# A group's residual moved into the next group's first step, and its token statistics spread over that group's later steps

## The chip, the core and the metric

The kernel runs on one core of a Trainium2 chip. Its time is the device time of one execution, in microseconds (us). Five engines work side by side and meet at semaphores: PE (TensorE, matmuls; its weight loads are listed as PEld), DVE (VectorE), ACT (ScalarE), POOL (GpSimd) and SP (SyncE, which here issues the DMAs).

## The reference

The model has two layers, each a gated cross attention and a gated feed-forward part, over x of 128 batches x 64 tokens x 128 features. The change lies in the feed-forward part of layer 0, a mixture of 16 experts in which each expert chooses 32 tokens of every batch:

```python
gates, idx = jax.lax.top_k(affinity, CAP)                 # CAP = 32 tokens per expert and batch
expert_in = jnp.take_along_axis(x[:, None, :, :], idx[..., None], axis=2)
h = jax.nn.gelu(jnp.einsum('becd,edf->becf', expert_in, w1) + b1[None, :, None, :])
expert_out = jnp.einsum('becf,efd->becd', h, w2) + b2[None, :, None, :]
out = out.at[jnp.arange(b)[:, None, None], idx].add(gates[..., None] * expert_out)
```

Around it stands `x = x + tanh(g_ffn[0]) * ffn(layernorm(x))`, and the attention of layer 1 begins with a layernorm of the new x.

## The kernel before

x stays on the chip as 64 tiles of 128 tokens. The expert stage, `run_experts`, cuts the 128 batches into 8 groups of 16 (8 tiles, 512 chosen rows for each expert). A group goes through the 16 experts one after another, so the stage is a pipeline of 128 steps. `body(a)` issues, on every engine, what belongs to one step `j`; `a.e` is the step's number in its group, from 1 to 16.

On PE a step has four parts, in this order: two `take` matmuls that gather rows of the next group (L1428, into `psR` and `psH`); 12 matmuls of the first layer of expert j+1 (L231, `psH`), called H here; 48 matmuls of the second layer of expert j (L231, `psE`), called E; and 16 that add the result of expert j-1 back to the tokens (L1503, `psA`), called A. In a group's first step eight matmuls seed `psA` with the bias (L1496). `psE` and `psA` have one buffer each.

On DVE a step is, in this order: a copy of gathered rows (L1582, `xg`); the gating of E's result, `psE` times the gate into `eo32` (L1615, semaphore `gated`); four `put` matrices (L1622); the low half of h (L1604); the low half of `eo` (L1630); and the other low half of h (L1604). Every second step also normalises a tile: L1563, L1577 and at its end L1568. ACT does the other copy of gathered rows, two pairs of Gelus (L1544) each followed by the high half of h (L1549), and the high half of `eo` (L1539).

Each engine takes its instructions in the order in which they are written, so three waits matter here. E of step j waits for `gated` of step j-1, because `psE` must be read before it is written again. A waits for `put` and `eo_lo`. The bias matmuls wait for `xadd`, which says that the group before has been read out of `psA`.

`residual(G)` runs on DVE alone, between step 16 of group G and step 1 of the next one. It waits for the group's last A, adds `psA` times the gate to the group's 8 tiles of x in two instructions (L1642), and then computes `bn_stats` for each of the 8 tiles (L176), which the layernorm of layer 1 will read after the stage.

`all_steps` writes steps -1 and 0 out, then loops over groups 0 to 5 (a `Fori` over G) with an inner loop of four steps a turn for steps 3 to 14, and writes groups 6 and 7 out (their inner loops stay). The last two groups gather little or nothing for a next one.

Of the kernel before, what the change touches and what calls it, by code (L numbers as in the profile page):

```python
# [24 lines left out]
NE, CAP, DFF = 16, 32, 512  # L25
# [78 lines left out]
def _build(nc, whole, I, out):  # L104
# [36 lines left out]
    x = sb(whole, "x", [P, NT, D], F32)  # L141
# [32 lines left out]
    def queue_stats(e, t):  # L174

        return e.bn_stats(tile_of(t, stats), tile_of(t, x))  # L176
# [1107 lines left out]
    def run_experts(tag, gate, ew, idx16, gate_slot, tok_slot):  # L1284
# [11 lines left out]
        GT = GB * N // P  # L1296
# [3 lines left out]
        with ExitStack() as c:  # L1300
# [71 lines left out]
                parity = (at.G + 1 + (at.k // GT if at.i is None else 0)) & 1  # L1372
                return [gathered(parity, at.bp, (k % GT if at.i is None else k) * 2 + side) for side in range(2)]

            def all_steps(eng, body, after_group):

                def group(G):
                    for k in (1, 2):
                        body(At(G, k))

                    fours = (NE - 4) // 4 - (isinstance(G, int) and G == NG - 2)
                    with eng.Fori(0, fours) as i:
                        for u in range(4):
                            body(At(G, 3 + u, i))
                    for k in range(3 + 4 * fours, NE + 1):
                        body(At(G, k))
                    after_group(G)
                for k in (-1, 0):
                    body(At(0, k))
                with eng.Fori(0, NG - 2) as G:  # L1390
                    group(G)
                for G in (NG - 2, NG - 1):
                    group(G)

            with nc.Block() as block:
# [23 lines left out]
                def _(e):  # L1419
# [25 lines left out]
                    def body(a):  # L1445
# [41 lines left out]
                        if a.has(-1):  # L1487
# [16 lines left out]
                                                        start=False,  # L1504
                                                        stop=a.e == NE and hl == 1, skip_group_check=True)
                            last.then_inc(s["A"], 1)
                    all_steps(e, body, lambda G: None)

                @block.scalar
                def _(e):  # L1510
                    for k in range(GT + 1):
                        t = Step(None, 0, k)
                        wait(e, s["ln"], t)
                        wait(e, s["g"], t - 2, 2)
                        e.activation(xn[:, k % 2, 0], xnf[:, k % 2], ACT.Copy).then_inc(s["x_hi"], 1)
                        if k < GT:
                            for hl in range(2):
                                wait(e, s["g"], t, 2, hl - 1)
                                e.activation(gathered(0, hl, 2 * k + 1),
                                             psH[:, 2 * hl + 1, :].rearrange("p (e c) -> p e c", c=CAP), ACT.Copy)\  # L1520
                                 .then_inc(s["g_1"], 1)

                    def body(a):
                        j, par = a.j, a.par

                        if a.has_tile(0):
                            wait(e, s["g"], a.t, 2, a.bp - 1)
                            e.activation(rows_of(a)[1], psH[:, 3, :].rearrange("p (e c) -> p e c", c=CAP), ACT.Copy)\
                             .then_inc(s["g_1"], 1)
                        for ft in range(FT):  # L1530
                            if ft == 2 and a.bp == 1 and a.has_tile(1):
                                tpar = (a.k + 1) % 2
                                wait(e, s["ln"], a.t + 1)
                                wait(e, s["g"], a.t - 1, 2)
                                e.activation(xn[:, tpar, 0], xnf[:, tpar], ACT.Copy).then_inc(s["x_hi"], 1)
                            if ft == 2 and a.has(-1):
                                wait(e, s["gated"], j - 1)
                                wait(e, seeded["A"], j - 2)
                                e.activation(eo[:, 0], eo32[:], ACT.Copy).then_inc(s["eo_hi"], 1)  # L1539
                            if a.has(1):  # L1540
                                wait(e, s["H"], j + 1, FT, ft + 1 - FT)
                                if ft % 2 == 0:
                                    wait(e, s["h_lo"], j, 2, ft // 2 - 1)
                                e.activation(g32[:, ft, :], psH[:, ft, :], ACT.Gelu_apprx_tanh,  # L1544
                                             bias=b1T[:, bass.ds(a.expert(1) * FT + ft, 1)]).then_inc(s["gelu"], 1)
                                if ft % 2 == 1:
                                    wait(e, s["gelu"], j + 1, FT, ft + 1 - FT)
                                    wait(e, s["E"], j - 1)
                                    e.activation(h[:, 1 - par, 0, ft - 1:ft + 1, :], g32[:, ft - 1:ft + 1, :],  # L1549
                                                 ACT.Copy).then_inc(s["h_hi"], 1)  # L1550
                    all_steps(e, body, lambda G: None)

                @block.vector
                def _(e):
# [6 lines left out]
                    def queue_tile(t, par):  # L1561
                        wait(e, s["x_lo"], t - 2)
                        e.tensor_scalar(xnf[:, par], tile_of(t, x), column_of(t, mean), column_of(t, rstd),  # L1563
                                        ALU.subtract, ALU.mult).then_inc(s["ln"], 1)
# [31 lines left out]
                    def body(a):  # L1596
                        j, par = a.j, a.par
                        next_tile = a.bp == 1 and a.has_tile(1)

                        def h_low(q):  # L1600
                            if a.has(1):
                                wait(e, s["h_hi"], j + 1, 2, q - 1)
                                wait(e, s["E"], j - 1)
                                e.tensor_tensor(h[:, 1 - par, 1, 2 * q:2 * q + 2, :], g32[:, 2 * q:2 * q + 2, :],  # L1604
                                                h[:, 1 - par, 0, 2 * q:2 * q + 2, :], ALU.subtract)\
                                 .then_inc(s["h_lo"], 1)

                        if a.has_tile(0):
                            gathered_rows(a.t, a.bp, rows_of(a)[0], psR[:])
                        if a.has(-1):  # L1610
                            wait(e, s["E"], j - 1)
                            wait(e, s["eo_lo"], j - 2)
                            g4 = gate_slot[:, bass.ds(a.expert(-1), 1), bass.ds(a.group(-1) * RT, RT)]\
                                .rearrange("p o r -> p (o r)")
                            e.tensor_tensor(eo32[:], psE[:], g4.unsqueeze(2).broadcast_to([P, RT, D]),  # L1615
                                            ALU.mult).then_inc(s["gated"], 1)
                        if next_tile:
                            queue_tile(a.t + 1, (a.k + 1) % 2)
                        if a.has(-1):
                            wait(e, seeded["A"], j - 2)  # L1620
                            for r in range(RT):
                                e.tensor_scalar(put[:, r, :], iota[:],  # L1622
                                                tok_slot[:, bass.ds(a.expert(-1), 1),
                                                         bass.ds(a.group(-1) * RT + r, 1)]
                                                .rearrange("p o r -> p (o r)"),
                                                None, ALU.is_equal).then_inc(s["put"], 1)
                        h_low(0)
                        if a.has(-1):
                            wait(e, s["eo_hi"], j - 1)
                            e.tensor_tensor(eo[:, 1], eo32[:], eo[:, 0], ALU.subtract)\  # L1630
                             .then_inc(s["eo_lo"], 1)
                        if next_tile:
                            select(a.t + 1, (a.k + 1) % 2, False)
                        h_low(1)
                        if next_tile:
                            split_tile(a.t + 1, (a.k + 1) % 2)

                    def residual(G):
                        wait(e, seeded["A"], At(G, NE - 1).j)
                        for q in range(2):  # L1640
                            xs = x[:].rearrange("p (t h) d -> p t h d", h=2)[:, bass.ds(G * RT, RT), q, :]
                            last = e.scalar_tensor_tensor(xs, psA[:, q], gate, xs, ALU.mult, ALU.add)  # L1642
                        last.then_inc(s["xadd"], 1)
                        wait(e, seeded["xadd"], flat(G, 1, None, 0, 0))
                        for k in range(GT):
                            queue_stats(e, flat(G, GT, None, 0, k))
                    all_steps(e, body, residual)
        s.close()


# [350 lines left out]
```

## Time and profile before

| | us |
|---|---|
| median of 3 runs | 2259.38 |
| lowest and highest | 2254.52 and 2264.16 |
| the profiled execution | 2259.92 |
| its span | 2258.2 |

The time of the profiled execution is 1.72 us longer than its span. In the page's list of busy time PE is busy for 2070.6 us (92% of the span), DVE for 1746.0 us (77%), ACT for 1598.8 us (71%) and POOL for 653.8 us (29%). The expert stage lies between about 575 and 1466 us. In the rows below an engine's start and duration are in us from the start of the span, and the granted clock of TensorE is a share of full speed, so 1.00 is 2.4 GHz and 0.50 is 1.2 GHz.

### The profile page before, as it was taken

Reading aid. Unit: us, or ns where it says so; the run is one execution under the profiler, and the core shown is the slowest. Engines: PE = TensorE matmul, PEld = TensorE weight load, DVE = VectorE, ACT = ScalarE, POOL = GpSimd, SP = SyncE. Lnnn points to the kernel's source line nnn. Section 1 sums busy time; section 2 is a strip of 40 time slices with the busy share of each in tenths; the row PEclk is TensorE's granted clock in tenths of the full one; section 3 lists DMA queues with packets and bytes.
Section 4 is the critical chain, followed back from the end, with each engine's and each line's share of the span. In section 5 each row is a group of like instructions: output and inputs, shape, how many; then the busy total and the mean of one; then the engine's idle time right before and its main releaser. Section 6 shows DMA issues by size and latency. Waiting matters only on the chain. (4 is left out here: it accounts for less than half of the span.)

```text
span 2258.2 us, 74593 instructions
## 1 busy us (share of the span) xinstructions
PE 2070.6 (92%) x26251; PEld 1394.0 (62%) x26251; DVE 1746.0 (77%) x3815; ACT 1598.8 (71%) x2792; POOL 653.8 (29%) x890
## 2 busy tenths in 40 slices
PE   6999999675799999999999999879999999999798
PEld 4666666433366666666666667656666666667566
DVE  4888887578787878787878787678888888888644
ACT  4777777454687888888878887656666667777533
POOL 3666666401000000000000000035455554444454
PEclk8999999777799999999999999989999999999899
DMA  7011110247000000000000000031111110000133
GB/s 173 27 32 31 32 32 26 53 172 279 12 10 11 9 11 12 10 11 11 9 11 9 12 8 2 0 91 61 58 57 59 60 52 7 4 4 5 41 103 103
DMA packets 105107, 96.64 MB, mean 43 GB/s; under 512 B 35920, under 2 KB 90048, under 8 KB 104640
## 3 DMA queue, kind: packets, MB, share of 16 engines
q1 hardware_dynamic: 104464, 95.51, 13.8%
q8 instruction: 45, 0.74, 0.1%
q14 instruction: 38, 0.31, 0.0%
q10 hardware_dynamic: 560, 0.08, 0.0%
HBM read 56.00 MB, written 31.10 MB: 39 GB/s over the span
## 5 line engine op out<-in xcount | busy, mean ns | idle before, releaser
L1604 DVE TENSOR_TENSOR h<-g,h 128x1024 f16<-128x1024 f32 x256 | 313.7, 1225 | 173.0 <-ACT h L1549 171.5
L231 PE MATMUL psE<-ew,h 128*128 (+1 forms) x6144 | 389.5, 223 | 31.7 <-DVE eo L1615 30.4
L231 PEld LDWEIGHTS psE<-ew,h 128*128 128x128 f16 x6144 | 370.9, 100 | 75.8 <-issue 28.8
L231 PE MATMUL psH<-xg,ew 128*128 (+1 forms) x1536 | 354.8, 381 | 2.4 <-issue 1.8
L1544 ACT ACTIVATE g<-psH,eb1T 128x512 f32<-128x512 f32 x512 | 322.5, 679 | 36.5 <-PE psH L231 27.0
L570 PE MATMUL psV<-Bw,cT 96*64 96x512 f16 x2064 | 288.0, 386 | 3.9 <-DVE vB L749 3.9
L723 POOL TENSOR_TENSOR E<-E,rden 128x512 f32<-128x512 f32 x192 | 200.4, 1044 | 292.6 <-DVE rden L758 292.6
L1549 ACT ACTIVATE h<-g 128x1024 f16<-128x1024 f32 x256 | 270.9, 1058 | 18.0 <-ACT g L1544 1.5
L714 POOL TENSOR_TENSOR Ph<-E,Ph 128x512 f16<-128x512 f32 x192 | 222.4, 1158 | 181.2 <-ACT Ph L674 181.2
L1662 POOL MEMSET rbias<- 64x384 f32 x1 | 0.4, 412 | 910.5 <-POOLq L132 910.5
L655 ACT ACTIVATE vB<-psV 128x512 f16<-128x512 f32 x344 | 202.9, 590 | 78.5 <-PE psV L570 78.5
L231 PEld LDWEIGHTS psH<-xg,ew 128*128 (+1 forms) x1536 | 144.0, 98 | 182.6 <-issue 35.2
L231 PE MATMUL psU<-cT,AT 96*128 96x128 f16 x3648 | 241.6, 222 | 13.3 <-DVE vB L749 11.9
L231 PEld LDWEIGHTS psU<-cT,AT 96*128 96x128 f16 x3648 | 208.9, 99 | 34.4 <-issue 11.2
L749 DVE TENSOR_TENSOR vB<-psV,vB 128x512 f16<-128x512 f32 x344 | 226.9, 659 | 0.4 <-ACT vB L655 0.4
L640 PE MATMUL psS<-u,xTa 128*64 128x256 f32 x1536 | 210.7, 396 | 2.0 <-ACT u L692 1.6
L692 ACT ACTIVATE u<-psU 128x512 f32<-128x512 f32 x304 | 180.8, 595 | 38.0 <-PE psU L231 30.8
L763 DVE COPY PT<-psT 128x1024 f16<-128x1024 f16 x192 | 132.4, 690 | 78.1 <-PE psT L627 77.9
L766 DVE TENSOR_REDUCE top<-psS 128x8 f32<-128x512 f32 x192 | 132.4, 690 | 64.3 <-PE psS L640 64.3
L606 PEld LDWEIGHTS psY<-vB,PT 128*64 128x64 f16 x4608 | 144.8, 110 | 34.3 <-DVE PT L763 11.8
L606 PE MATMUL psY<-vB,PT 128*64 128x128 f16 x4608 | 163.1, 220 | 1.6 <-DVE PT L763 1.6
L686 ACT ACTIVATE E<-E,zero_col 128x512 f32<-128x512 f32 x192 | 138.3, 720 | 25.5 <-DVE E L769 25.5
(253 smaller groups left out, 3121.0 us busy)
## 6 DMA issues: line engine op xcount, KB each, us to landing
keys_ahead<-ust SPq DMA_DIRECT2D x40, 512.0 KB, 4.8
u<-keys_ahead SPq DMA_DIRECT2D x40, 512.0 KB, 3.4
rawe<-in_L_ffn_w_dram SPq DMA_DIRECT2D x32, 256.0 KB, 2.7
wb<-rw SPq DMA_DIRECT2D x64, 128.0 KB, 2.0
rows<-places SPq DMA_DIRECT2D x110, 64.0 KB, 2.6
out_dram<-x SPq DMA_DIRECT2D x7, 512.0 KB, 3.2
context_T<-cT SPq DMA_DIRECT2D x64, 48.0 KB, 1.5
cT<-context_T SPq DMA_DIRECT2D x64, 48.0 KB, 1.7
```

Of the source, the lines that this page charges most:

```text
L231: last = e.matmul(to, a, b, start=start and n == 0, stop=stop and n == 2, **flags)
L570: last = e.matmul(a.values(b)[half(hp)], cT[:, a.ring, cl, half(b)], Bw[:, bl, a.g, hp].rearrange("p k d -> p (k d)"), start=n == 0, stop= ...
L606: last = e.matmul(psY[half(b), 0:D], PT[:, a3.par, pl, pair, half(b)], vB[:, a3.par, vl, b, pair, :], start=a3.g == n == pair == 0, stop=a ...
L640: last = e.matmul(psS[half(b), h:h + 4, :], xT[:, a.tp, half(b)], u[:, a.slot, h:h + 4, half(b)], start=True, stop=True)
L655: e.activation(vB[:, a.par, 0, b].rearrange("p k d -> p (k d)"), a.values(b), ACT.Copy).then_inc(s["vh" + name], 1)
L692: e.activation(u[:, a.slot, 4 * b:4 * b + 4].rearrange("p h l -> p (h l)"), psU[:, b, :], ACT.Copy).then_inc(s[f"uc{b}"], 1)
L714: e.tensor_tensor(Ph[:, a2.par, 1].rearrange("p k t -> p (k t)"), E[:, a2.par].rearrange("p h l -> p (h l)"), Ph[:, a2.par, 0].rearrange(" ...
L723: e.tensor_tensor(E[:, a1.par], E[:, a1.par], rden[:, a1.par, :].unsqueeze(2).broadcast_to([P, 8, N]), ALU.mult)\
L749: e.tensor_tensor(vB[:, a.par, 1, b].rearrange("p k d -> p (k d)"), a.values(b), vB[:, a.par, 0, b].rearrange("p k d -> p (k d)"), ALU.sub ...
L1544: e.activation(g32[:, ft, :], psH[:, ft, :], ACT.Gelu_apprx_tanh, bias=b1T[:, bass.ds(a.expert(1) * FT + ft, 1)]).then_inc(s["gelu"], 1)
L1549: e.activation(h[:, 1 - par, 0, ft - 1:ft + 1, :], g32[:, ft - 1:ft + 1, :], ACT.Copy).then_inc(s["h_hi"], 1)
L1604: e.tensor_tensor(h[:, 1 - par, 1, 2 * q:2 * q + 2, :], g32[:, 2 * q:2 * q + 2, :], h[:, 1 - par, 0, 2 * q:2 * q + 2, :], ALU.subtract)\
```

## The change

`residual` is split in two. The additions to x for group G-1 now stand in step 1 of group G, behind that step's gating (L1615) and ahead of its `put` instructions. The eight statistics of group G-1 stand at the end of later steps of group G: two at the end of step 2, and one each at the end of steps 3, 5, 7, 9, 11 and 13. After the last group both parts run as before. Since group 0 has no group before it, its steps are written out ahead of the loop, which now runs over groups 1 to 5.

```diff
-            def all_steps(eng, body, after_group):
+            def all_steps(eng, body):
...
-                    after_group(G)
                 for k in (-1, 0):
                     body(At(0, k))
-                with eng.Fori(0, NG - 2) as G:
+                group(0)
+                with eng.Fori(1, NG - 2) as G:
                     group(G)
...
                         if next_tile:
                             queue_tile(a.t + 1, (a.k + 1) % 2)
+                        if a.e == 1 and a.i is None and not (a.fixed and a.G == 0):
+                            residual(a.G, -1)
                         if a.has(-1):
                             wait(e, seeded["A"], j - 2)
...
+                        if not (a.fixed and a.G == 0):
+                            if a.e == 2 and a.i is None:
+                                group_stats(a.G, -1, None, (0, 1))
+                            elif 3 <= a.e <= 14 and a.e % 2 == 1:
+                                group_stats(a.G, -1, a.i, (2 + (a.e - 3) // 2,))
-
-                    def residual(G):
-                        wait(e, seeded["A"], At(G, NE - 1).j)
+
+                    def residual(G, off):
+                        wait(e, seeded["A"], flat(G, NE, None, 0, NE * off + NE - 1))
                         for q in range(2):
...
                             last = e.scalar_tensor_tensor(xs, psA[:, q], gate, xs, ALU.mult, ALU.add)
                         last.then_inc(s["xadd"], 1)
-                        wait(e, seeded["xadd"], flat(G, 1, None, 0, 0))
-                        for k in range(GT):
-                            queue_stats(e, flat(G, GT, None, 0, k))
-                    all_steps(e, body, residual)
+
+                    def group_stats(G, off, i, tiles):
+                        wait(e, seeded["xadd"], flat(G, 1, None, 0, off))
+                        for k in tiles:
+                            queue_stats(e, flat(G, GT, i, 2, GT * off + k))
+
+                    all_steps(e, body)
+                    residual(NG - 1, 0)
+                    group_stats(NG - 1, 0, None, range(GT))
```

This is DVE's queue in the kernel before where group 6 ends and group 7 begins; `eo_1` is the tile `eo32`, and `x` from `psA` is the residual.

```order
1164 L1604 TENSOR_TENSOR h<-g_1,h 128x1024
1165 L1642 SCALAR_TENSOR_TENSOR x<-psA,tanh_g,x 128x4x128 x2
1166 L176 BN_STATS stats<-x 128x6 x8
1167 L1615 TENSOR_TENSOR eo_1<-psE,gate_slot 128x512
1168 L1622 TENSOR_SCALAR put<-iota,tok_slot 128x128 x4
1169 L1604 TENSOR_TENSOR h<-g_1,h 128x1024
1170 L1630 TENSOR_TENSOR eo<-eo_1,eo 128x512
```

And this is the same place in the changed kernel, with the number of the line moved to L1650 for the residual and L1624 for `put`.

```order
1291 L1604 TENSOR_TENSOR h<-g_1,h 128x1024
1292 L1615 TENSOR_TENSOR eo_1<-psE,gate_slot 128x512
1293 L1650 SCALAR_TENSOR_TENSOR x<-psA,tanh_g,x 128x4x128 x2
1294 L1624 TENSOR_SCALAR put<-iota,tok_slot 128x128 x4
1295 L1604 TENSOR_TENSOR h<-g_1,h 128x1024
1296 L1632 TENSOR_TENSOR eo<-eo_1,eo 128x512
```

The gating has moved ahead of the two additions, and the eight statistics have left this place; the additions stand ahead of `put` and of the low half of `eo`.

The second place is the end of step 2 and the beginning of step 3 of a group inside the loop, in DVE's queue of the changed kernel.

```order
966 L1604 TENSOR_TENSOR h<-g_1,h 128x1024
967 L81 REGISTER_ALU
968 L1568 TENSOR_TENSOR xne<-xnfe,xne 128x128
969 L81 REGISTER_ALU
970 L176 ISA
971 L176 REGISTER_ALU
972 L176 BN_STATS stats<-x 128x6
973 L176 ISA
974 L176 REGISTER_ALU
975 L176 BN_STATS stats<-x 128x6
976 L1382 UNCONDITIONAL_BRANCH
```

Two statistics, with their register instructions, have come in between the last instruction of step 2 and the inner loop, where step 3 begins with `xg` and the gating.

## Rows read from the trace of the kernel before

**Rows 1.** Waits, 700 to 1470 us: us in total, times, longest.
```profile
PE psE L231 <- DVE eo L1615: 30.0, 20, 4.2
```
**Rows 2.** Timeline, end of group 0: start, us, engine, line, operation, [idle before <-releaser].
```profile
706.27 0.38 PE L1428 MATMUL psR<-sel,xne 64*128 64x512 f16 x1
...
706.62 2.76 PE L231 MATMUL psH<-xg,ew 128*128 x12
...
707.77 1.40 DVE L1642 SCALAR_TENSOR_TENSOR x<-psA,tanh_g,x 128x512 f32 x2
...
709.36 1.91 DVE L176 BATCH_NORM_STATS2 stats<-x  x8 [0.18 <-DVE x L1642]
712.19 0.69 DVE L1582 CAST xg<-psR 128x512 f32 x1 [0.92 <-issue]
712.80 0.68 DVE L1615 TENSOR_TENSOR eo<-psE,gate_slot 128x512 f32<-128x512 f32 x1
...
713.54 5.30 PE L231 MATMUL psE<-ew,h 128*128 128x128 f16 x48 [4.16 <-DVE eo L1615]
...
714.04 1.22 DVE L1604 TENSOR_TENSOR h<-g,h 128x1024 f16<-128x1024 f32 x1
...
715.18 0.69 DVE L1630 TENSOR_TENSOR eo<-eo,eo 128x512 f16<-128x512 f32 x1
```
**Rows 3.** The seven boundary steps on PE: stretch, length, PE busy (instructions), clock.
```profile
706.27:719.46 13.19, 9.03 (x87) 0.74 0.03 11
...
1364.25:1374.50 10.25, 7.89 (x89) 0.83 0.01 2
sum 84.19, PE 58.55; mean PE 8.36
```
**Rows 4.** Other stretches on PE, same columns.
```profile
601.49:608.36 6.87, 6.62 (x89) 1.00 0.08 20
713.54:718.78 5.24, 5.24 (x50) 0.51 0.00 0
593.97:595.79 1.82, 0.00 (x1) 1.00 0.00 0
739.10:745.55 6.45, 6.25 (x79) 1.00 0.06 20
```
**Rows 5.** Timeline, PE from the bias on, two boundaries.
```profile
718.78 0.40 PE L1496 MATMUL psA<-eb,weigh 48*128 48x128 f16 x8
...
719.46 0.38 PE L1428 MATMUL psR<-sel,xne 64*128 64x512 f16 x1
...
1369.37 4.14 PE L231 MATMUL psE<-ew,h 128*128 128x128 f16 x48 [2.36 <-DVE eo L1615]
```
**Rows 6.** Timeline, DVE where the inner loop turns back.
```profile
753.48 0.28 DVE L1568 TENSOR_TENSOR xne<-xnfe,xne 128x128 f16<-128x128 f32 x1
753.69 0.68 DVE L1582 CAST xg<-psR 128x512 f32 x1
```
**Rows 7.** Timeline, gating and E of steps 3, 5, 6 and 8, and H.
```profile
728.08 0.68 DVE L1615 TENSOR_TENSOR eo<-psE,gate_slot 128x512 f32<-128x512 f32 x1
...
728.92 3.19 PE L231 MATMUL psE<-ew,h 128*128 x48
...
742.06 3.10 PE L231 MATMUL psE<-ew,h 128*128 x48 [0.20 <-DVE eo L1615]
...
747.12 0.68 DVE L1615 TENSOR_TENSOR eo<-psE,gate_slot 128x512 f32<-128x512 f32 x1
...
748.46 2.84 PE L231 MATMUL psE<-ew,h 128*128 x48
...
758.99 2.76 PE L231 MATMUL psH<-xg,ew 128*128 x12
...
760.71 0.68 DVE L1615 TENSOR_TENSOR eo<-psE,gate_slot 128x512 f32<-128x512 f32 x1
...
761.59 3.03 PE L231 MATMUL psE<-ew,h 128*128 x48
```

More of the change, by code:

```diff
@@ L1506, in body @@
                             last.then_inc(s["A"], 1)
-                    all_steps(e, body, lambda G: None)
+                    all_steps(e, body)
                 @block.scalar
@@ L1550, in body @@
                                                  ACT.Copy).then_inc(s["h_hi"], 1)
-                    all_steps(e, body, lambda G: None)
+                    all_steps(e, body)
                 @block.vector
@@ L1636, in body @@
                             split_tile(a.t + 1, (a.k + 1) % 2)
-                    def residual(G):
-                        wait(e, seeded["A"], At(G, NE - 1).j)
+                        if not (a.fixed and a.G == 0):
[5 more added lines that the diff above has]
+                        wait(e, seeded["A"], flat(G, NE, None, 0, NE * off + NE - 1))
                         for q in range(2):
-                            xs = x[:].rearrange("p (t h) d -> p t h d", h=2)[:, bass.ds(G * RT, RT), q, :]
+                            xs = x[:].rearrange("p (t h) d -> p t h d", h=2)\
+                                [:, bass.ds(flat(G, RT, None, 0, RT * off).value, RT), q, :]
                             last = e.scalar_tensor_tensor(xs, psA[:, q], gate, xs, ALU.mult, ALU.add)
                         last.then_inc(s["xadd"], 1)
-                        wait(e, seeded["xadd"], flat(G, 1, None, 0, 0))
-                        for k in range(GT):
-                            queue_stats(e, flat(G, GT, None, 0, k))
-                    all_steps(e, body, residual)
+                    def group_stats(G, off, i, tiles):
+                        wait(e, seeded["xadd"], flat(G, 1, None, 0, off))
+                        for k in tiles:
+                            queue_stats(e, flat(G, GT, i, 2, GT * off + k))
+                    all_steps(e, body)
+                    residual(NG - 1, 0)
+                    group_stats(NG - 1, 0, None, range(GT))
         s.close()
```

## The prediction

> **What bounds the kernel now.** I read the page first: PE is busy for 92% of the span, so only what leaves PE idle or slow can be worth much. In the list of waits for the expert stage, PE's wait in front of E for the gating instruction on DVE comes to 30.0 us in 20 cases, the longest 4.2 us [rows 1]. The timeline at the end of group 0 shows where it arises [rows 2]. H began at 706.62; where nothing is awaited E follows H's start by 761.59 - 758.99 = 2.60 us [rows 7], so PE is ready for E at 709.22. E needs `psE` read out by the gating, and DVE comes to that only after the two residual additions (707.77), the eight statistics (709.36 to 711.27), an idle 0.92 us and the copy of gathered rows (712.19). The gating starts at 712.80, and E at 713.54, after 4.16 us of idle. Then E itself takes 5.30 us.
>
> The windows on PE tell the second half. The granted clock in that E is 0.51, so PE is at 1.2 GHz, and it had been idle before it fell [rows 4]. The seven boundary steps, counted from one take to the next, sum to 84.19 us with 58.55 us of PE busy [rows 3]. Step 1 of group 0 does the same work without a residual, at a clock of 1.00: 6.87 us, of which PE is busy for 6.62 [rows 4]. Seven such steps would be busy for 46.3 us, so 58.55 - 46.3 = 12.2 us of the boundary time is the low clock, and the rest of the surplus (84.19 - 7 x 6.87 = 36.1 us in all) is idle.
>
> **The change part by part: a boundary step.** DVE's work doesn't shrink; its order does. I replay the first boundary from the take at 706.27 as zero [rows 2].
> - The first instruction behind step 16 started at 1.50 (707.77). It was the residual and is now the copy `xg`, and the gating follows one pitch (712.80 - 712.19 = 0.61) later at 2.11; it ends at 2.79.
> - E could start 0.35 + 2.60 = 2.95 after the take by PE's own work. The gating's end and the 0.06 us that passed between its end and E's start (713.48 to 713.54) make 2.85. E starts at 2.95 at once, and the 4.16 us are gone.
> - The residual's wait, for the group's last A, stands in front of `put`, which waits for that A anyway. So the wait adds nothing. The two additions start at 2.70 and hold DVE for some 1.34 us (1.40 in the row, less the overlap with the next). From gating to h's low half it was 714.04 - 712.80 = 1.24 us, and is now 1.24 + 1.34, which puts it at 4.69; the low half of `eo` follows 1.14 later at 5.83 and ends at 6.52.
> - PE ends E at 2.95 + 2.84 = 5.79 (the duration at full clock, as in step 6 [rows 7]) and must wait for that low half: bias and A now begin at about 6.62. From the bias to the next take it is 719.46 - 718.78 = 0.68 us [rows 5]. The step takes 7.30 us.
>
> So the wait is not gone; it is turned into a smaller one in front of the bias, some 0.6 us beyond what group 0's step has. Queued behind the additions on DVE are only `put`, the halves of h and `eo`; ACT's next Gelus need the h half by the next step, by which time it's done (5.83).
>
> The last boundary (1364.25) has no take, no `xg` and no split. H's start is the zero, the gating follows step 16's last instruction at about 1.30 (an estimate: 1.50 less the 0.35 of the missing take, and something for the order on ACT), the low half of `eo` ends 4.41 later, as above (6.52 - 2.11), at 5.71, and the next H starts about 0.8 us after that, at 6.50. The seven together: 6 x 7.30 + 6.50 = 50.3 us. **Saved: 84.19 - 50.3 = 33.9 us**, which includes the 12.2 us of low clock. I count the clock as given back, because an idle of 0.6 us is left where there were 2.36 to 4.16 us [rows 2, 5], and a gap of 1.82 us ahead of group 0 shows a granted clock of 1.00 all through [rows 4].
>
> I let the idle 0.92 us ahead of `xg` vanish. It stands where the outer loop turns back, directly behind eight short statistics. At the inner loop's turn, behind a long instruction, `xg` follows the split after 0.21 us with no idle at all [rows 6], and after the change the outer turn looks like that one. The bound on the other side: if it stays on the four turns that are left, the gating is 0.92 us late, E by about 0.8 us, 3.3 us in all. I take nothing, the nearer row.
>
> On what a turn costs, the Trainium skill ("Runtime: NRT & Kernel Launch", section "Instruction fetch mechanics") says that a taken branch to a target outside the loaded window stalls for a fetch. The inner turn shows none; the 0.92 us at the outer one may be it. By that rule the four turns would keep their idle, and the sum would be the 3.3 us smaller.
>
> **The statistics.** Each is worth a pitch of 1.91/8 = 0.24 us on DVE [rows 2], and each now stands right in front of the next step's copy and gating, for which E waits. What hides it is the slack between the end of the gating and the moment at which PE is through H.
> - Step 3 (after two statistics, 0.48 us): the gating ends at 728.76 and E starts at 728.92, with no slack. Cost 0.48.
> - Step 6: the gating ends at 747.80, E starts at 748.46, slack about 0.6. Steps 4, 10 and 14 are of its kind. Cost nothing; uncovered it would be 0.24.
> - Step 8: the gating ends at 761.39 and E starts at 761.59; less 0.13 for the semaphore (step 5: 741.93 to 742.06), the slack is 0.07. Cost 0.17; step 12 is its like.
>
> The rows for step numbers are in [rows 7]. A group costs 0.48 + 2 x 0.17 = 0.82 us, over six groups **4.9 us**. In group 7 there are no takes or copies, and the slack covers it. The bounds: nothing, if PE's neighbouring delays absorb them, and 8 x 0.24 x 7 = 13.4 us, if each one is on the path.
>
> **The rest.** Group 0 written out loses some register instructions and is fetched once more; its first pass in the old loop shows a step of 6.87 us with nothing remarkable, so nothing on either side, up to 1 us. Matmuls, ACT, DMAs and their waits stay as they are. The tail after group 7 is the same, and the next stage starts behind a barrier, so what the stage gains the kernel gains.
>
> **Sum.** 33.9 - 4.9 = 29.0 us off the profiled execution's 2259.92: **2231 us**. Against the median of the runs, 2259.38, which is 0.5 us away from the profiled one, that is -1.3%.
>
> **The rivals.**
> 1. The clock still falls at the boundaries. For it: it has fallen in every one so far, even after 2.36 us of idle [rows 5], and a shorter one is left. Against it: 1.82 us without a fall [rows 4]. Price: the 12.2 us stay, time 2243. The Trainium skill ("TensorE: Matmul & The Clock Gate", section "A second HAM failure mode: psum-queue depth-cycling") says that frequent short idles between matmul groups can make the clock oscillate too. By that rule it would be this rival.
> 2. Every statistic lands on the path: 13.4 instead of 4.9 us, time 2239.4. For it: steps 3 and 5 already wait for the gating [rows 7]. Against it: steps such as 6 with 0.6 us to spare.
> 3. Better than forecast: the statistics are absorbed and the residual's 0.6 us as well. Then 36 us, time 2224.
> 4. Slower than before. The mechanism is the clock in the ordinary steps: a delayed E leaves PE idle several times a group, and the clock drops there as it does at the boundaries. A drop costs 12.2/7 = 1.7 us. To end 11.3 us slower, it must eat 29.0 + 11.3 = 40.3 us, 24 drops, more than three in each group. Against it: step 5 already waits for the gating, and its window shows a clock of 1.00 [rows 4, 7]. Time from 2271.
> 5. Nothing comes of it: the code that is new in the program, or a wait that the trace of before doesn't show, takes the 29.0 us back. The first pass through the old loop, in group 0, speaks against it: its step of 6.87 us is no longer than the work in it [rows 4]. Time 2259.
>
> **How the numbers follow.** 0.5% of 2259 is 11.3 us, about what a measurement of this kernel can tell from no change; faster means under 2248. Chances: the forecast 0.55 (2226 to 2237), the clock 0.13, all statistics 0.13, better 0.12, slower 0.03, nothing 0.04. The first four are all under 2248; I take 0.04 off them for where the clock's and the statistics' cases lie near that line. Faster 0.89, same 0.08, slower 0.03. The range takes in the better case, the clock's and the statistics' case: 2223 to 2244.
>
> **What would show it.** In the profile after, the seven boundary steps should last 7.3 us (the last 6.5) at a clock of 1.00, with E directly behind H, 0.6 to 0.9 us of idle ahead of the bias released by the low half of `eo`, and no idle of 0.9 us at the outer turn. The waits of E for the gating should fall from 30.0 us to under 10, with the largest ones at step 3. If E after the boundary takes 4 us or more, the first rival holds; if E starts late in all even steps, the second; if the boundary steps are right and the time isn't, the loss is in the ordinary steps.

## The result and the profile after

The changed kernel takes 2227.6 us (median of 4 runs, 2224.11 to 2228.16), the kernel before 2257.76 us in the same comparison. The ratio is 0.986, with a 95% interval of 0.9835 to 0.9885: faster by 1.4%. 2231 us was forecast, which is 3.4 us above the median. The profiled execution has a span of 2225.3 us against 2258.2, so 32.9 us less.

The first view is the list of waits of the changed kernel for 700 to 1440 us (us in total, times, longest). It answers [rows 1].

```profile
PE psE L231 <- DVE eo L1615: 6.0, 15, 2.1
PE psA L1496 <- DVE eo L1632: 5.3, 5, 1.1
...
PE psA L1496 <- issue: 1.1, 2, 0.8
```

PE's wait in front of E has fallen from 30.0 to 6.0 us, of which 2.1 are one wait at the end of the stage, in step 16 of group 7; the kernel before has the same 2.1 us there. A wait that was not there has come: the bias matmuls wait for the low half of `eo`, five times and 1.1 us at most. The last two boundaries have such a wait too, 0.81 and 0.33 us, which the list puts under "issue". The timeline at the end of group 0, all engines, stands against [rows 2].

```profile
703.11 0.38 PE L1428 MATMUL psR<-sel,xne 64*128 64x512 f16 x1
...
703.45 2.76 PE L231 MATMUL psH<-xg,ew 128*128 x12
703.48 1.22 DVE L1604 TENSOR_TENSOR h<-g,h 128x1024 f16<-128x1024 f32 x1 [0.87 <-ACT h L1549]
...
704.83 0.68 DVE L1582 CAST xg<-psR 128x512 f32 x1
705.43 0.68 DVE L1615 TENSOR_TENSOR eo<-psE,gate_slot 128x512 f32<-128x512 f32 x1
...
706.03 1.40 DVE L1650 SCALAR_TENSOR_TENSOR x<-psA,tanh_g,x 128x512 f32 x2
...
706.16 2.85 PE L231 MATMUL psE<-ew,h 128*128 128x128 f16 x48
...
707.34 0.73 DVE L1624 TENSOR_SCALAR put<-iota,tok_slot 128x128 f16<-128x128 f16 x4
707.99 1.22 DVE L1604 TENSOR_TENSOR h<-g,h 128x1024 f16<-128x1024 f32 x1
...
709.12 0.68 DVE L1632 TENSOR_TENSOR eo<-eo,eo 128x512 f16<-128x512 f32 x1
...
710.14 0.40 PE L1496 MATMUL psA<-eb,weigh 48*128 48x128 f16 x8 [1.12 <-DVE eo L1632]
```

E starts 2.71 us after H, where it had started 6.92 us after it, and takes 2.85 us in place of 5.30. It ends at about 709.0, and DVE, whose chain now runs gating, two additions, `put`, h, `eo`, ends that chain at 709.80. The idle 1.12 us runs from E's end to the bias at 710.14; the last 0.34 us of it lie behind the end of `eo`. The windows on PE over the seven boundary steps answer [rows 3] (stretch, length, PE busy, granted clock).

```profile
703.11:710.82 7.71, 6.59 (x91) 1.00 0.08 19
...
1334.94:1341.50 6.56, 6.23 (x89) 1.00 0.02 4
sum 51.93, PE 45.34; mean PE 6.48
```

The clock is 1.00 in each, and the seven sum to 51.93 us in place of 84.19. The stretches of 15 steps between them, groups 1 to 6, are the next two fences, first of the kernel before and then of the changed one.

```profile
719.46:817.16 97.70, 96.03 (x1176) 1.00 0.04 10
...
sum 584.04, PE 574.34; mean PE 95.72
```

```profile
710.82:808.98 98.16, 96.52 (x1176) 1.00 0.04 11
...
sum 586.46, PE 576.81; mean PE 96.13
```

They have grown by 2.42 us. Group 0 and what follows the last boundary are the last two, again before and after.

```profile
601.49:706.27 104.78, 102.67 (x1258) 1.00 0.04 12
1374.50:2258.20 883.70, 829.84 (x11254) 0.98 0.14 45
```

```profile
599.24:703.11 103.87, 102.14 (x1259) 1.00 0.04 12
1341.50:2225.30 883.80, 832.69 (x11253) 0.97 0.14 45
```

The account of the 32.9 us is then: boundary steps -32.26, groups 1 to 6 +2.42, group 0 -0.91, the rest of the kernel +0.10, and -2.25 before group 0 (601.49 to 599.24). That last part can't be put down to the change: in the other profiles below group 0 starts anywhere from 597.89 to 601.48 us. Without it the kernel has gained 30.65 us in the profile, against 29.0 forecast and 30.2 by the medians.

### The profile page after: what moved, and what is told of

The parts are those of the page before. It is cut to its first block and busy times, and to the rows that moved or that the text cites. A ratio compares the mean times of both kernels' runs of the same rounds, so it can differ in the third digit from the quotient of the medians.

```text
span 2225.3 us, 74451 instructions
## 1 busy us (share of the span) xinstructions
PE 2061.3 (93%) x26251; PEld 1382.5 (62%) x26251; DVE 1740.4 (78%) x3815; ACT 1595.8 (72%) x2792; POOL 653.7 (29%) x890
## 5 line engine op out<-in xcount | busy, mean ns | idle before, releaser
L231 PEld LDWEIGHTS psE<-ew,h 128*128 128x128 f16 x6144 | 360.3, 98 | 54.1 <-issue 29.0
L231 PE MATMUL psE<-ew,h 128*128 (+1 forms) x6144 | 380.6, 219 | 7.8 <-DVE eo L1615 7.2
```

The lines of the kernel that those rows point to most:

```text
L231: last = e.matmul(to, a, b, start=start and n == 0, stop=stop and n == 2, **flags)
```

## The experiments

Each run is timed against the kernel before. The three comparisons gave that kernel medians of 2258.25 us (the first four experiments), 2256.34 (the next three and the dose of 8) and 2259.46 (the doses of 12 and 16). The changed kernel was not run again beside them, so a difference from its 2227.6 us is one between comparisons: the intervals of the ratios are about 0.002 wide to either side, 5 us, and below that only the profiles decide.

**Group 0 written out, nothing else** (the kernel before with this edit):

```diff
-                with eng.Fori(0, NG - 2) as G:
+                group(0)
+                with eng.Fori(1, NG - 2) as G:
```

> The kernel before, with group 0 written out ahead of the loop and nothing else. My theory (the gain comes from the order on VectorE at the seven boundaries): no change, ratio to before 1.000 within 0.002, the boundary steps still 10 to 13 us long. Rival (writing a group out gives part of the gain, since group 0 ran 0.9 us faster in the changed kernel): 1 to 3 us faster.

2253.42 us (2245.8 to 2261.36, 10 runs), ratio 0.9977, interval 0.9964 to 0.9991: 2 to 8 us faster, 5.2 in the middle. My expectation of no change was wrong; the rival, 1 to 3 us, had the sign right and was probably too small. The profile is of its fastest execution, 2243.9 us of span; PE at the first boundary and one later one:

```profile
707.90 2.85 PE L231 MATMUL psE<-ew,h 128*128 128x128 f16 x48 [3.03 <-DVE eo L1616]
...
816.02 4.38 PE L231 MATMUL psE<-ew,h 128*128 128x128 f16 x48 [3.78 <-DVE eo L1616]
```

Written out, the first boundary has no loop to turn, its statistics need no registers (1.64 us for the eight in place of 1.91), and PE's idle falls from 4.16 to 3.03 us. In this execution the clock held there: that step takes 9.58 us, in place of 13.19. The other six still idle for 2.34 to 3.78 us ahead of E and have a slow E; together they are 2.4 us shorter, of which 1.6 lie in the fifth, where E happened to be slow for 5.30 us before and for 4.10 here. In these two profiles this is 3.6 us at the first boundary and 1.0 us in group 0. The profile is a lucky one, 7.6 us under the median of the ten runs, so a usual execution may gain less than these 3.6 us at the first boundary.

**Gating first, statistics together** (the changed kernel; the spread statistics go, and all eight follow the additions):

```diff
                             residual(a.G, -1)
+                            group_stats(a.G, -1, None, range(GT))
...
-                        if not (a.fixed and a.G == 0):
-                            if a.e == 2 and a.i is None:
-                                group_stats(a.G, -1, None, (0, 1))
-                            elif 3 <= a.e <= 14 and a.e % 2 == 1:
-                                group_stats(a.G, -1, a.i, (2 + (a.e - 3) // 2,))
```

> The changed kernel, with the eight statistics directly behind the two additions in the group's first step instead of spread. My theory: E starts on time, and the low half of eo comes 8 x 0.24 us = 1.9 us later, so a boundary step takes 7.53 + 1.95 = 9.5 us; the ordinary steps win back the 0.4 us a group that the spread statistics cost. In all 7 x 1.95 - 2.4 = 11.2 us slower than the changed kernel, 2239, if the clock stays at full speed in the idle of 3.0 us that now stands ahead of the bias. Rival (the clock falls with it): up to 1.3 us more a boundary, 2248. If the place of the statistics made no difference, 2228.

2247.28 us, ratio 0.9953 (0.9937 to 0.997). This is the rival's number. PE at the first boundary:

```profile
705.86 2.85 PE L231 MATMUL psE<-ew,h 128*128 128x128 f16 x48
712.00 0.40 PE L1496 MATMUL psA<-eb,weigh 48*128 48x128 f16 x8 [3.29 <-DVE eo L1633]
712.24 0.62 PE L1503 MATMUL psA<-eo,put 64*128 64x128 f16 x16
712.68 0.38 PE L1428 MATMUL psR<-sel,xne 64*128 64x512 f16 x1
713.00 4.45 PE L231 MATMUL psH<-xg,ew 128*128 x12
```

E is on time and the idle has moved behind it, in front of the bias, 3.29 us long; and the clock falls in the next H, which takes 4.45 us in place of 2.76. It fell so behind five of the seven boundaries. The seven steps sum to 66.42 us, as the theory had it (7 x 9.5); the slow H behind them is the rest. Without the spreading, putting the gating first is worth 11 us against the kernel before, of which about 5 came with group 0.

**Additions ahead of the gating, statistics spread** (the changed kernel, with the additions back at the start of the step):

```diff
+                        if a.e == 1 and a.i is None and not (a.fixed and a.G == 0):
+                            residual(a.G, -1)
                         if a.has_tile(0):
                             gathered_rows(a.t, a.bp, rows_of(a)[0], psR[:])
```

> The changed kernel, with the two additions at the very beginning of the first step, ahead of the copy and the gating, as before the change; the statistics stay spread. E starts 1.3 us later than in the changed kernel (idle about 1.3 us ahead of it), and the low half of eo is no later than now. If the clock holds: step 0.35 + 2.60 + 1.3 + 2.84 + 0.27 + 0.68 = 8.0 us against 7.53, 7 x 0.5 = 3.5 us slower, 2231. Rival (any idle ahead of E lowers the clock, as at all seven boundaries before): each E takes 1.2 to 2.5 us more, 2243.

2229.01 us, ratio 0.987 (0.9853 to 0.9886), which can't be told from the changed kernel's 0.986. PE and DVE at the first boundary:

```profile
707.86 2.85 PE L231 MATMUL psE<-ew,h 128*128 128x128 f16 x48 [1.36 <-DVE eo L1617]
...
709.50 0.68 DVE L1632 TENSOR_TENSOR eo<-eo,eo 128x512 f16<-128x512 f32 x1
...
710.64 0.40 PE L1496 MATMUL psA<-eb,weigh 48*128 48x128 f16 x8
```

The idle stands ahead of E once more, 1.36 us, and none ahead of the bias. `eo` is done at 710.18 and the bias follows E at 710.64, so here the step ends with the chain additions, gating, E, and in the changed kernel with the chain gating, additions, `put`, h, `eo`. The two happen to be nearly equally long, because E takes PE 2.85 us, and `put`, h and `eo` take DVE 2.4 us, with another 0.34 before the bias. The clock holds at all seven boundaries, so the rival falls. The seven steps sum to 53.51 us against 51.93. The gating's new place, which the forecast made the heart of the matter, is thus worth 1.6 us once the statistics are gone from there, less than the runs can tell. Moving the statistics away is worth 24 us by itself: the run with only group 0 written out took 2253.42 us in the same comparison.

**Without the statistics of groups 0 to 6** (the spread ones are left out altogether, so the layernorm of the next stage reads unset values):

> The changed kernel without the statistics of groups 0 to 6 (left out altogether; only the last group's are computed, so the next stage's layernorm reads unset ones). It prices the spread statistics. From the two profiles an ordinary stretch of 15 steps grew by 0.33 to 0.49 us a group: 2.4 us faster than the changed kernel, 2225. By the prediction's working, 0.82 us a group and nothing in group 7: 4.9 us faster, 2222.7. If all eight lay on the path: 13.4 us, 2214.

2226.18 us, ratio 0.9861 (0.9843 to 0.988). That is 1.4 us under the changed kernel by the medians, within what these runs can tell. The windows are sharper. This is the stretch of group 2 in it, 97.71 us, where the changed kernel has 98.10 and the kernel before 97.77:

```profile
815.56:913.27 97.71, 96.08 (x1178) 1.00 0.03 10
```

Over groups 1 to 6 the stretches sum to 583.94 us, against 586.46 in the changed kernel. So the eight statistics cost 0.4 us a group, 2.5 us in all, and the prediction's 0.82 a group is out.

**Statistics in DVE's gap** (the changed kernel; the same lines, ahead of the last low half of h):

```diff
                         if next_tile:
                             select(a.t + 1, (a.k + 1) % 2, False)
+                        if not (a.fixed and a.G == 0):
+                            ...
                         h_low(1)
```

> The changed kernel, with each spread statistic moved from the end of its step to just ahead of the step's last low half of h, where VectorE has stood idle for 0.9 us waiting for ScalarE. My theory (a statistic costs time only where it stands between that half and the next step's gating): the 15 ordinary steps of a group fall back from 98.1 to 97.7 us, 2.4 us faster than the changed kernel in all, 2225. Rival (VectorE's total work counts, not the place): unchanged, 2227.6. In steps with a tile to select the gap may be too short for two statistics: then step 2 keeps some of its cost.

2225.27 us, ratio 0.9856 (0.9833 to 0.9879). The median is 2.3 us under the changed kernel's, as expected, though the interval alone would not show it. The profile does, in group 2's stretch on PE and in DVE's timeline of step 2:

```profile
815.98:913.65 97.67, 96.02 (x1178) 1.00 0.03 10
```

```profile
716.48 0.48 DVE L176 BATCH_NORM_STATS2 stats<-x  x2
717.43 1.23 DVE L1604 TENSOR_TENSOR h<-g,h 128x1024 f16<-128x1024 f32 x1 [0.47 <-ACT h L1549]
```

Two statistics fill a part of the gap in which DVE waits for ACT, 0.47 us of it is left, and the stretch is back at its old length; the six stretches sum to 584.05 us, before 584.04. The place counts, not the sum of DVE's work.

**Low half of `eo` first** (the changed kernel; in a group's first step only):

```diff
-                        h_low(0)
+                        late = a.e == 1 and a.i is None and not (a.fixed and a.G == 0)
+                        if not late:
+                            h_low(0)
                         if a.has(-1):
                             wait(e, s["eo_hi"], j - 1)
...
+                        if late:
+                            h_low(0)
```

> The changed kernel, with the low half of eo ahead of the first low half of h in a group's first step, directly behind put. My theory (the 1.04 us of idle ahead of the bias is the length of VectorE's chain gating, residual, put, h, eo): eo is ready 1.14 us earlier, the bias follows E with only 0.27 us between, the boundary step falls from 7.53 to about 6.8 us (6.2 for the last), 7 x 0.75 = 5 us faster, 2222.5. Rival (ScalarE's high half of eo, or its next Gelus waiting for the h half, take over): less than 2 us, 2226 or more.

2221.41 us (2220.57 to 2221.66), ratio 0.9832 (0.981 to 0.9854). That is 6.2 us under the changed kernel's median, and in the profiles the seven boundary steps sum to 45.12 us against 51.93, 6.8 less. PE and DVE at the first boundary:

```profile
708.37 2.85 PE L231 MATMUL psE<-ew,h 128*128 128x128 f16 x48
...
710.20 0.68 DVE L1634 TENSOR_TENSOR eo<-eo,eo 128x512 f16<-128x512 f32 x1
...
711.21 0.40 PE L1496 MATMUL psA<-eb,weigh 48*128 48x128 f16 x8
```

`eo` is done at 710.88, before E is, and the bias follows E directly. The step takes 6.58 us (705.31 to 711.89) instead of 7.71. This shows that the 1.12 us of idle was the length of DVE's chain. Now E is what ends the step, so the gating's place should matter again: with the additions ahead of it E began 1.4 us later in the third experiment. The two edits were not run together.

**Both edits together.**

> Both edits of the two runs before: statistics in the gap and eo first. If they are independent the gains add: 2.4 + 5 = 7.4 us faster than the changed kernel, 2220, ratio to before 0.983. If both draw on the same slack of VectorE, one of the two gains: 2222 to 2225.

2218.17 us (2216.84 to 2219.93, 5 runs), ratio 0.9821 (0.9802 to 0.984): the fastest version, 9.4 us under the changed kernel's median and 1.8% under the kernel before. The gains add: the seven boundary steps sum to 45.10 us and the six stretches to 583.95, each as in the run that had its edit alone.

**Idle put back in doses.** The last three runs are the changed kernel with n additional statistics of a constant tile ahead of the gating in each group's first step, n = 8, 12 and 16:

```diff
+                        if a.e == 1 and a.i is None and not (a.fixed and a.G == 0):
+                            for k in range(n):
+                                e.bn_stats(pad[:, k], ident32[:])
                         if a.has(-1):
                             wait(e, s["E"], j - 1)
```

> The changed kernel with eight additional statistics (of a constant tile, into a scratch tile; extra work, nothing left out) ahead of the gating in a group's first step. They put back 1.7 to 1.9 us of idle ahead of E at each boundary. If idle time alone counts: 7 x 1.9 - 7 x 0.3 (what was slack) = about 11 us slower than the changed kernel, 2239, E still 2.84 us long. Rival (an idle of some 2 us ahead of E lowers the clock, as 2.36 us did in the kernel before): E 4 us or more at the boundaries, 1.7 us more each, 2251.

> As the run with eight additional statistics, but twelve: idle of some 2.4 us ahead of E and 1.1 us ahead of the bias. Eight cost 12 us and the clock held in their profile. If idle time alone counts: another 7 x 4 x 0.21 = 6 us, 2246. Rival (the clock falls at an idle of this length, as it did after 2.34 us at the last boundary of the kernel before): E 4 us or more at the boundaries, some 1.5 us more each, 2256.

> Sixteen additional statistics: idle of some 3.2 us ahead of E. Idle alone: 2252. With the low clock at every boundary: 2262. The two runs together show whether the cost bends between an idle of 1.5 and one of 3.2 us.

| added | median us | ratio to before (interval) | idle ahead of E in the profile | boundaries with a slow E |
|---|---|---|---|---|
| 0 (changed kernel) | 2227.6 | 0.986 (0.9835 to 0.9885) | none | 0 of 7 |
| 8 | 2239.85 | 0.9917 (0.9895 to 0.994) | 0.90 to 1.69 | 0 of 7 |
| 12 | 2245.65 | 0.9941 (0.9924 to 0.9957) | 1.68 to 2.46 | 2 of 7 |
| 16 | 2253.17 | 0.997 (0.9957 to 0.9982) | 2.45 to 3.24 | 4 of 7 |

The three medians, 2239.85, 2245.65 and 2253.17 us, stand beside 2239, 2246 and 2252, the numbers for idle time alone. The profile of the run with 16 is the second fastest of its nine executions, so the median one may have had more slow boundaries than four. The clock does fall more often as the idle grows, but the length alone doesn't decide. Two boundaries of the run with 12, with the same 2.08 us of idle:

```profile
926.57 4.48 PE L231 MATMUL psE<-ew,h 128*128 128x128 f16 x48 [2.08 <-DVE eo L1619]
930.99 0.40 PE L1497 MATMUL psA<-eb,weigh 48*128 48x128 f16 x8
...
1034.92 2.85 PE L231 MATMUL psE<-ew,h 128*128 128x128 f16 x48 [2.08 <-DVE eo L1619]
1038.90 0.40 PE L1497 MATMUL psA<-eb,weigh 48*128 48x128 f16 x8 [1.12 <-DVE eo L1636]
```

They also show why a fall is cheap here. The slow E is 1.6 us longer, but the bias comes 4.42 us after E's start in the one and 3.98 in the other: the 1.12 us for which PE waits for `eo` is hidden under the slow E. A fall costs 0.44 us there, and 0.2 to 0.4 at the three middle boundaries of the run with 16. In the kernel before nothing was there to hide it: `eo` ended at 715.87 [rows 2] and the slow E only at 718.78 [rows 5].

## Why the prediction was right, and where it wasn't

- **What bounds the boundary** was right: the chain on DVE in front of the gating, and the low clock behind it. All seven steps have a clock of 1.00 now, as forecast, with idles of 0.33 to 1.12 us ahead of the bias, so the first rival falls. The Trainium skill ("TensorE: Matmul & The Clock Gate", section "A second HAM failure mode: psum-queue depth-cycling") tells of frequent short idles that make the clock oscillate; these seven, one in about 100 us, did not.
- **The boundary steps**: 50.3 us forecast, 51.93 measured; saved 32.3 against 33.9. Two small terms were short. From the end of `eo` to the bias I had put 0.1 us; it is 0.33 to 0.34 at the five boundaries whose next group runs in the loop (709.80 to 710.14 at the first) and 0.10 at the sixth (1238.12 to 1238.22). And the chain on DVE ran 0.2 to 0.3 us later than copied at the first and the sixth; at the four between them the low half of `eo` ended 6.51 to 6.52 us after the take, where 6.52 was forecast.
- **The idle at the loop's turn** vanished, as taken. At the turns E follows H as directly as elsewhere, and a boundary without a turn (the first experiment) has no such idle. The 0.92 us were those of the first turn; the other four turns of the kernel before idled 0.62 us each, so the bound of 3.3 us was too high for the four that are left. Whether a fetch or register work made this idle stays open; no run separates them.
- **The statistics**: 4.9 us forecast, 2.4 measured. This is the term that was mis-sized. The delays in steps 8 and 12 were right (0.17), the one in step 3 is 0.38 where I had put 0.48, and the sum was wrong in the main because I added each in full. PE in steps 8 and 9 of group 1 of the changed kernel:

```profile
750.73 2.76 PE L231 MATMUL psH<-xg,ew 128*128 x12
753.50 3.12 PE L231 MATMUL psE<-ew,h 128*128 x48
...
757.32 2.76 PE L231 MATMUL psH<-xg,ew 128*128 x12
759.96 3.10 PE L231 MATMUL psE<-ew,h 128*128 x48
```

  E of step 8 starts 2.77 us after its H, 0.17 late, exactly the 0.17 of the working. But E of step 9 is only 0.04 late (2.64), where in the kernel before that step was late by 0.31 of its own (its H at 765.32, its E at 768.23). It makes the loss good: from H of step 8 to H of step 10 it is 13.03 us, before 13.02. Steps 12 and 13 do the same. What stays is mostly step 3, ahead of which two statistics stand; it grew from 6.64 to 6.99 us.
- **The reason given for the gain** was half wrong. The forecast put it down to the gating coming ahead of the additions. The third experiment has the additions ahead again and loses 1.6 us in the profile. What counts is that the statistics left DVE's chain before the group's first A: with all eight back in it, behind the gating, 20 us of the 30 are gone. In the profile the steps themselves are 14.5 us longer and the slow H behind five of them add about 7, less the 2.5 that the spread statistics cost.
- **Group 0 written out** was put at nothing, up to 1 us. By itself it is worth 2 to 8 us; inside the whole change only the 0.9 us in group 0 comes on top, since its first boundary is among the seven steps that were already counted.
- **The sum** came within 2 us of the 30.65 of the profile in part by luck: the boundary steps saved 1.6 us less than forecast, and the statistics (2.5 us) and group 0 (0.9 us) made up for it.
- **The other rivals**: all statistics on the path (13.4 us) is refuted by the run without them, and slower and nothing by the result. Of the rivals the better case came nearest in time (2224 forecast, 2227.6 measured), but not for its reason: the residual's idle stayed and was even larger.

## What to carry to other kernels

When work is moved off a pipeline's critical instruction, follow the engine's whole chain to the step's last consumer: here gating and additions could be swapped for 1.6 us, because E and DVE's rest of the chain are about equally long, and the real gains were to take out of the chain what nobody in that step needs (the statistics, and then the first low half of h). Put such work into a gap that the trace shows on that engine, in front of an instruction that waits for another engine, and not right behind it. And count small delays with the neighbouring steps' own slack, or they add up to twice what they cost.

## What was not expected of the hardware

TensorE's clock fell to the lower level after idles of 2.08 to 4.16 us ahead of E, and held through others of 2.02 to 3.05 us in kernels that also had falls; with 0.90 to 1.69 us it fell at none of the seven boundaries of one profile. With the idle ahead of the bias (the second experiment) it fell after 2.01 and after 3.22 to 3.29 us and held through 2.49 and 3.13. So between about 2 and 3.3 us the length of the idle alone doesn't tell, and what decides there stays open. The execution of the kernel with group 0 written out that kept the clock at its first boundary is also the fastest of ten, and that kernel's time spreads more (2245.8 to 2261.36 us over 10 runs) than that of the fastest version (2216.84 to 2219.93 over 5). The mean granted clock of those ten executions mostly falls as their time grows: 0.962 in the fastest, 0.951 in the slowest. That the clock's falls at the boundaries make this spread is likely and was not shown, since only one of the ten has a profile.
